# One-core perceiver layer: the passage from attention to the experts reordered, with seven tiles' routing tables made on GpSimd

## The reference

```python
p1 = jnp.cumsum(m1, axis=-2) - m1              # place among those that chose the same expert first
m1 = m1 * (p1 < C)
p2 = jnp.cumsum(m2, axis=-2) - m2 + m1_count   # second choices come behind the first ones
m2 = m2 * (p2 < C)
combine = c1 + c2                              # (token, expert, slot): the gate, 0 elsewhere
dispatch = (combine != 0)
expert_inputs = einsum('GSEC,GSM->EGCM', dispatch, x)
hidden = gelu(expert_inputs @ w0) * (expert_inputs @ w1)      # 1368 wide
out = einsum('EGCM,GSEC->GSM', hidden @ wo, combine)
```

## Time and profile before

| | |
|---|---|
| median of 3 runs (lowest, highest) | 552.87 us (552.48, 552.99) |
| the profiled execution | 554.64 us, span 552.5 us |
| granted TensorE clock, mean share | 0.944 |
| TensorE busy | 498.8 us, 90% of the span |
| VectorE, ScalarE, GpSimd busy | 400.5, 324.6, 254.5 us |

### The profile page before, as it was taken

The page is one execution under the profiler, slowest core; times in us unless marked ns, Lnnn a source line. Parts: engine busy times, 40 slices in busy tenths (PEclk is TensorE's granted clock), DMA queues, the critical chain, the costliest instruction groups (busy, mean ns, idle before and its releaser), DMA issues.

```text
span 552.5 us, 18285 instructions
## 1 busy us (share of the span) xinstructions
PE 498.8 (90%) x6637; PEld 457.4 (83%) x6637; DVE 400.5 (72%) x1003; ACT 324.6 (59%) x839; POOL 254.5 (46%) x349
## 2 busy tenths in 40 slices
PE   0888999999999999999966747999999999999996
PEld 0776888888888888888755536899999999999995
DVE  2444555666767766676777697599999999999963
ACT  1356777667757775775731216666666666666650
POOL 4134345344364344536310110566676666667650
PEclk9989999999999999999996655699999999999998
DMA  6623211201101110100017000344655656457202
GB/s 163 182 77 89 42 40 31 54 21 43 41 20 38 39 39 19 39 20 3 3 45 264 1 1 0 114 145 165 192 160 166 212 191 189 126 185 229 79 1 76
DMA packets 58125, 48.91 MB, mean 89 GB/s; under 512 B 20942, under 2 KB 49744, under 8 KB 58064
## 3 DMA queue, kind: packets, MB, share of 16 engines
q1 hardware_dynamic: 58064, 48.09, 30.3%
HBM read 46.86 MB, written 1.08 MB: 87 GB/s over the span
## 4 chain that ended last, share of the span: by engine, by line
PE 79%; ACT 5%; issue 5%; DVE 5%; DMA 3%; SPq 2%; ACTq 0%; DVEq 0%
PE bank L222 20%; PE bank L224 18%; PE bank L223 18%; PE bank L605 5%; PE bank L629 3%; PE bank L583 3%; PE bank L540 2%; ACT Pr L1058 2%; DMA w_raw<-in_L_xattn_Wk 2%; PE bank L760 2%; PE bank L988 2%; SPq L417 1%; ACT PTd L1151 1%; DMA last_prob<-Pr 1%; PE bank L722 1%
## 5 line engine op out<-in xcount | busy, mean ns | idle before, releaser
L222 PE MATMUL bank<-XT_lo,W_hi 128*128 128x256 f32 (+1 forms) x352 | 100.7, 286 | 1.3 <-ACT CT L1252 1.3
L223 PE MATMUL bank<-XT_hi,W_lo 128*128 128x256 f32 (+1 forms) x352 | 100.2, 285 | 0.0
L224 PE MATMUL bank<-XT_hi,W_hi 128*128 128x256 f32 (+1 forms) x352 | 100.0, 284 | 0.0
L2001 POOL TENSOR_TENSOR W_lo<-raw,W_hi 128x256 fp32r<-128x256 f32 (+1 forms) x88 | 87.8, 998 | 7.0
L1919 POOL TENSOR_TENSOR Pr<-Pr 128x1024 f32<-128x1024 f32 x31 | 58.8, 1897 | 48.8 <-DVE Pr L1401 48.0
L1058 ACT ACTIVATE Pr<-Sc,nmax 128x257 f32<-128x257 f32 x128 | 63.8, 502 | 23.1 <-DVE nmax L1392 20.1
L1392 DVE CUSTOM_DVE_ANT_0 Sc<-bank,mask_add 128x257 f32<-128x257 f32 x128 | 47.0, 423 | 40.3 <-PE bank L583 18.0
L1999 POOL CAST W_hi<-raw 128x256 fp32r<-128x256 f32 (+1 forms) x88 | 39.4, 447 | 75.0 <-PE bank L224 38.0
L1817 DVE TENSOR_TENSOR W_lo<-raw,W_hi 128x512 fp32r<-128x512 f32 (+1 forms) x88 | 69.6, 793 | 5.1 <-ACT W_hi L1225 1.4
L1847 DVE TENSOR_TENSOR hid_lo<-hid,hid_hi 128x256 fp32r<-128x256 f32 (+1 forms) x88 | 71.9, 818 | 1.5 <-ACT hid_hi L1301 1.5
L222 PEld LDWEIGHTS bank<-XT_lo,W_hi 128*128 128x128 f32 (+1 forms) x352 | 66.7, 190 | 1.6 <-issue 1.6
(11 more groups left out here) (238 smaller groups left out, 1331.3 us busy)
## 6 DMA issues: line engine op xcount, KB each, us to landing
raw<-in_L_ffn_w_kernel SPq DMA_DIRECT2D x32, 512.0 KB, 4.6
ctx_raw<-in_ctx SPq DMA_DIRECT2D x32, 256.0 KB, 2.8
raw<-in_L_ffn_wo_kernel SPq DMA_DIRECT2D x16, 512.0 KB, 5.7
raw<-in_L_ffn_w_kernel SPq DMA_DIRECT2D x16, 344.0 KB
last_prob<-Pr SPq DMA_DIRECT2D x128, 1.0 KB
raw<-in_L_ffn_wo_kernel SPq DMA_DIRECT2D x8, 256.0 KB
x_sb<-in_x SPq DMA_DIRECT2D x4, 256.0 KB, 6.4
VL_all<-vl_rows SPq DMA_DIRECT2D x8, 128.0 KB
```

The lines of the kernel that those rows point to most:

```text
L222: pe.matmul(dst, a_hi, b_lo, start=first, stop=False)
L223: pe.matmul(dst, a_lo, b_hi, start=False, stop=False)
L224: return pe.matmul(dst, a_hi, b_hi, start=False, stop=last)
L2001: po.tensor_tensor(W2_lo[0:w, m % RW, :], raw2[0:w, t, :], f(W2_hi[0:w, m % RW, :]), ALU.subtract)\
```

## The change

The calls of the stretch are put in another order on TensorE, VectorE, ScalarE and GpSimd, and several pieces of work change their engine or their bank. By parts:

- `normalise_last` goes into the last step of the loop, right behind `spread_probs` of tile 5; ScalarE multiplies two of the four groups and VectorE two. Before, VectorE multiplied all four after the loop.
- The values of tiles 6 and 7 are projected into a bank of their own (`self_values_at`), so that they need not wait for the rotation to have read queries and keys; `project_self(y_, True)` goes into the loop's last step.
- `spread_probs(y_)` is made by ScalarE alone, in four blocks; `scale_probs(y_)` goes from VectorE to GpSimd.
- Tiles 5 and 6 are chosen and placed together, in the form that tiles 0 to 4 had (`shift_group`, `share_group`, `choose_group`, `leave_first`, `place_group`); tile 7 keeps the single form.
- `add_weights(t)` on GpSimd takes the place of `weigh(t)` and `disperse(t)` for tiles 0 to 6. VectorE keeps both for tile 7. There are four `disp` buffers in the place of two.
- The turning of the weights of tiles 4 to 7 goes behind the first products of the feed-forward, and VectorE copies the low inputs of tile 7.

```diff
+        def add_weights(t):
+            po.wait_ge(sm["r_placed"], group_of(t) + 1)
+            if t >= 1:
+                po.wait_ge(sm["r_weighed"], t)
+            po.tensor_scalar(halves_[:, :], slot_no, slot_of[:, 1, one(t)], gate[:, 1, one(t)], ALU.is_equal, ALU.mult)
+            po.tensor_scalar(tile_of(C_all, t), slot_no, slot_of[:, 0, one(t)], gate[:, 0, one(t)], ALU.is_equal, ALU.mult)\
+              .then_inc(sm["r_halves"], 1)
+            po.wait_ge(sm["r_halves"], t + 1)
+            po.tensor_tensor(tile_of(C_all, t), tile_of(C_all, t), halves_[:, :], ALU.add).then_inc(sm["r_weighed"], 1)
+            po.wait_ge(sm["r_weighed"], t + 1)
+            if t >= 4:
+                po.wait_ge(sm["r_x_made"], t - 3)
+            po.tensor_scalar(disp_of(t), tile_of(C_all, t), 0.0, None, ALU.is_gt).then_inc(sm["r_disp"], 1)
...
         def normalise_last():
+            ve.wait_ge(sm["p_normed"], B - 1)
             ve.wait_ge(sm["p_inv"], B)
             r = (B - 1) % 2
-            ve.tensor_tensor(Pr[:, r, :, 0:2 * P], Pr[:, r, :, 0:2 * P], Pr[:, r, :, SC:SC + 1].broadcast_to([P, G, 2 * P]),
+            ve.tensor_tensor(Pr[:, r, 2:G, 0:2 * P], Pr[:, r, 2:G, 0:2 * P], Pr[:, r, 2:G, SC:SC + 1].broadcast_to([P, G - 2, 2 * P]),
                              ALU.mult).then_inc(sm["p_normed"], 1)
...
+        def normalise_last():
+            ac.wait_ge(sm["p_normed"], B - 1)
+            ac.wait_ge(sm["p_inv"], B)
+            r = (B - 1) % 2
+            for g in range(2):
+                last = ac.activation(Pr[:, r, g, 0:2 * P], Pr[:, r, g, 0:2 * P], ACT.Copy, scale=Pr[:, r, g, SC:SC + 1])
+            last.then_inc(sm["p_normed"], 1)
...
+                    if isinstance(j, int) and j == TT - 1:
+                        project_self(j - 1, True)
...
         turn_qk(z)
+        scores(z)
         self_outputs(y_)
-        scores(z)
...
+        def self_values_at(t):
+            return bk[5][:, D:2 * D] if isinstance(t, int) and t >= TT - 2 else bk[6][:, 0:D]
...
-            if t > 0:
-                ve.wait_ge(sm["r_weighed"], t)
             ve.tensor_scalar(second[:, :], slot_no, slot_of[:, 1, one(t)], gate[:, 1, one(t)], ALU.is_equal, ALU.mult)
...
-        for n in range(3):
-            split(0, n)
+        split(0, 0)
+        keep_low_inputs(z)
+        split(0, 1)
+        split(0, 2)
...
         up(*place(1))
+        turn_weights_of(2)
         for m in range(ALL):
             up(*place(m + 2))
             down(*place(m))
+            if m == 0:
+                turn_weights_of(3)
```

More of the change, by code:

```diff
@@ L685, in project_self @@
                 return
-            if of_values:
+            if of_values and isinstance(t, int) and t == TT - 2:
+                pe.wait_ge(sm["v_ready"], B)
+            elif of_values and isinstance(t, int) and t == TT - 1:
+                pe.wait_ge(sm["a_lT"], TT)
+            elif of_values:
                 pe.wait_ge(sm["b_cos"], t + 1)
@@ L701, in turn_qk @@
             pe.wait_ge(sm["b_rope"], t + 1)
[L702 removed]
+            if not isinstance(t, int) or t < TT - 2:
+                pe.wait_ge(sm["b_v"], t + 1)
             for i in range(4):
@@ L968, in down @@
                     pe.wait_ge(sm[by], max(EQ * half_ + q, 1))
+                if half_ == 0 and q == 1:
+                    pe.wait_ge(sm["ct_read"], 4)
             for h in range(SP_):
@@ L1149, in spread_probs @@
                 ac.wait_ge(sm["b_oT_made"], t)
-            for b in range(2):
+            for b in range(blocks):
                 last = ac.activation(PTd[b * S:(b + 1) * S, :, :, b, :],
@@ L1198, in step @@
                     keep_logits(j - 3)
+                if u == 3 and isinstance(j, int) and j == TT - 1:
+                    normalise_last()
                 keep_probs(b - 1, (u - 1) % 4)
@@ L1542, in spread_probs, with chain, follow @@
             last.then_inc(sm["b_pT_dve"], 1)
-        def chain(t, n, ins):
+        def chain(n, ins):
             ins.then_inc(sm["r_dve"], 1)
-            ve.wait_ge(sm["r_dve"], PICK * (t - EARLY) + n)
-        def follow(t, n, ins):
+            ve.wait_ge(sm["r_dve"], n)
+        def follow(n, ins):
             ins.then_inc(sm["r_slot"], 1)
-            ve.wait_ge(sm["r_slot"], PLACE * (t - EARLY) + n)
+            ve.wait_ge(sm["r_slot"], n)
         count = [0]
@@ L1605, in place_early @@
                                             op0=ALU.is_lt, op1=ALU.mult))
+            ve.sem_inc(sm["r_placed"], 1)
         def read_logits(t):
@@ L1614, in choose @@
         def choose(t):
-            ve.wait_ge(sm["r_neg"], t - EARLY + 1)
+            ve.wait_ge(sm["r_neg"], 1)
             first, last = lowest[:, 0, one(t)], lowest[:, 1, one(t)]
-            chain(t, 1, ve.scalar_tensor_tensor(out=tile_of(pick, t), in0=tile_of(lg, t), scalar=least[:, one(t)], in1=expert_no,
+            chain(1, ve.scalar_tensor_tensor(out=tile_of(pick, t), in0=tile_of(lg, t), scalar=least[:, one(t)], in1=expert_no,
                                                 op0=ALU.is_equal, op1=ALU.mult))
-            chain(t, 2, ve.tensor_reduce(first, tile_of(pick, t), X, ALU.min))
+            chain(2, ve.tensor_reduce(first, tile_of(pick, t), X, ALU.min))
@@ L1621, in choose @@
             ve.tensor_scalar(tile_of(chosen[:, 0], t), expert_no, first, None, ALU.is_equal)
-            ve.wait_ge(sm["r_exp"], t - EARLY + 1)
-            chain(t, 3, ve.scalar_tensor_tensor(out=tile_of(rest, t), in0=expert_no, scalar=first, in1=tile_of(exps_, t),
+            ve.wait_ge(sm["r_exp"], 1)
+            chain(3, ve.scalar_tensor_tensor(out=tile_of(rest, t), in0=expert_no, scalar=first, in1=tile_of(exps_, t),
                                                 op0=ALU.not_equal, op1=ALU.mult))
-            chain(t, 4, ve.tensor_reduce(gate[:, 1, one(t)], tile_of(rest, t), X, ALU.max))
@@ L1626, in choose @@
-            chain(t, 5, ve.scalar_tensor_tensor(out=tile_of(pick, t), in0=tile_of(rest, t), scalar=gate[:, 1, one(t)],
+            chain(4, ve.tensor_reduce(gate[:, 1, one(t)], tile_of(rest, t), X, ALU.max))
+            chain(5, ve.scalar_tensor_tensor(out=tile_of(pick, t), in0=tile_of(rest, t), scalar=gate[:, 1, one(t)],
                                                 in1=expert_no, op0=ALU.is_equal, op1=ALU.mult))
-            chain(t, 6, ve.tensor_reduce(last, tile_of(pick, t), X, ALU.min))
+            chain(6, ve.tensor_reduce(last, tile_of(pick, t), X, ALU.min))
@@ L1641, in slots_of @@
+            follow(2, ve.tensor_tensor(tile_of(pos2, t), at_[:, E:2 * E], tile_of(pos2, t), ALU.add))
             ve.sem_inc(sm["turns_ve"], 1)
@@ L1649, in slots_of @@
                                     op0=ALU.mult, op1=ALU.add)
[L1650 removed]
+            follow(4, ve.scalar_tensor_tensor(out=both(gate), in0=both(place_), scalar=float(CAP), in1=both(gate),
                                                  op0=ALU.is_lt, op1=ALU.mult))
         def weigh(t):
[L1655 to L1657 removed]
             ve.tensor_scalar(second[:, :], slot_no, slot_of[:, 1, one(t)], gate[:, 1, one(t)], ALU.is_equal, ALU.mult)
[L1659 removed]
+            follow(5, ve.tensor_scalar(tile_of(C_all, t), slot_no, slot_of[:, 0, one(t)], gate[:, 0, one(t)],
                                         ALU.is_equal, ALU.mult))
[L1661 removed]
+            ve.tensor_tensor(tile_of(C_all, t), tile_of(C_all, t), second[:, :], ALU.add).then_inc(sm["r_slot"], 1)
         statistics(0)
@@ L1705, in step @@
                     add_and_norm(j - 1, "b", 0)
+                ending = isinstance(j, int) and j == TT - 1
+                if ending and u == 3:
+                    invert_sums(B - 1, u)
+                    normalise_last()
+                    rotate(j - 1)
                 keep_probs(b - 1, (u - 1) % 4)
@@ L1709, in step @@
                 elif u == 3:
-                    rotate(j - 1)
+                    if not ending:
+                        rotate(j - 1)
                     split_self(j - 2)
```

274 lines of the change are left out of this document (140 added, 134 removed).

## The result

The change took 547.43 us (median of 16 runs) where the kernel before took 552.93 (16 runs): a ratio of 0.9909, 95% interval 0.9890 to 0.9929, or 5.0 us (3.9 to 6.1). The ratio is estimated from the runs in the chip's faster state and is not the quotient of the two medians, which is 0.9901. The forecast was 10.1 us. The sign is right and the time lies in the wide range of 537.0 to 549.5, but outside the forecast's own range of 539 to 546, and half of the gain is missing. The profiled execution took 548.07 us with a span of 546.3 (before 552.5).

A forecast was written before the change was run, and what follows sets the result against it. VectorE's queue was taken to bound the stretch before the feed-forward, with GpSimd idle beside it. First product 11.7 us earlier, less 1.6 given back, makes 10.1: 552.87 to 542.8 us; own range 539 to 546, wide range 537.0 to 549.5.

The forecast's parts named there:

- (a): Last block's probabilities at the loop's end: their turn on TensorE goes from 283.78 to about 280.8, 3.0 us earlier.
- (b): Cross projection of tile 7 on TensorE starts at 287.6 instead of 289.97, 2.4 us earlier.
- (c): Scores of tile 7 at 301.7 instead of 305.90, 4.2 us earlier; GpSimd's first weights start near 303.
- (d): Sum of tile 7 on VectorE at 315.0, 4.6 us earlier; its norm at 317.2, 6.6 us earlier.
- (e): Router's end on VectorE: places of tiles 5 and 6 at 326.8, with 2.0 us added for a busy GpSimd.
- (f): Weights and table on GpSimd: four steps of 0.72, 2.9 us a tile (1.9 to 3.9); last table at 332.6.
- (g): Last table to first feed-forward product: 3.4 us instead of 4.73, so the product at 336.0, 11.7 us earlier.
- (h): Turnings of tiles 4 to 7, now between the feed-forward's matrix products, give back 1.6 us.
- rival in which GpSimd becomes the bound: First product at 311 + 7w, w being GpSimd's us per tile; kernel slower from w = 5.0; chance 0.09.
- VectorE held up: Router's two-tensor VectorE steps lose 0.47 each beside GpSimd; (e) grows by 7.5 instead of 2.0; 548.3 us; chance 0.15.

## Why the forecast was half right

Each step of the forecast beside the row after; the last column adds the 1.1 us by which the loop ended earlier.

| step | forecast | measured | + 1.1 |
|---|---|---|---|
| (a) turn of the last probabilities | 280.8 | 279.36 | 280.5 |
| (b) cross projection of tile 7 | 287.6 | 286.29 | 287.4 |
| (c) scores of tile 7; first weights | 301.7; 303 | 300.99; 302.29 | 302.1; 303.4 |
| (d) sum of tile 7; its norm | 315.0; 317.2 | 314.77; 319.38 | 315.9; 320.5 |
| (e) places of tiles 5 and 6 | 326.8 | 327.95 | 329.1 |
| (f) a tile on GpSimd; last table | 2.9; 332.6 | 4.2; 337.59 | 338.7 |
| (g) from there to the first product | 3.4; 336.0 | 3.2; 340.80 | 341.9 |
| (h) turnings given back | 1.6 | 0.7 | |

(a) to (c) and the sum of tile 7 hold within 0.9 us: the order brings what it was to bring. That the stretch with all tables on VectorE is shorter by the same 11.7 us that the forecast had for the first product is a coincidence; the forecast's 11.7 has seven tables on GpSimd in it.

(f) is the step that failed, by the size of one term, the price of a tile on GpSimd. I had three rows and took the two-input step of the same size, 0.72; the two weight steps took 1.23 and 1.22 and the table step 0.86, each of them above it. The sum 1.23 + 1.22 + 0.73 + 0.86, with the gaps, is 4.2, beyond even the upper bound of 3.9. The Trainium skill (GPSIMD Engine Reference, 4.1 Engine selection) has one-input work at roughly line rate on GpSimd; these rows disagree: GpSimd took 1.23 for a step that VectorE wrote in 0.41. The nearest row was no neighbour in kind: a compare with a multiplication is not a cast, and no row of before had a scalar step at all.

The rest follows from the price. The late norm in (d) and the places in (e) come of it, since the power stood behind tile 2's weights; I had named this wait, for 3.9 us a tile. (e) itself was too long by 1.0: from the norm to the places it had 9.6 us and 8.6 were measured, with some 1.6 for the busy GpSimd where it had 2.0. With the power earlier the places were done at 325.98, on time. But that was not what the end waited for: at 2.9 a tile, the queue was to be free at 324, ahead of the places; at 4.2 it is free 0.9 behind them, and from there two tiles take 8.7 us instead of 5.8. GpSimd begins when the forecast said, at 302.29, and from there its queue has hardly a gap: the end is its sum. So with the 1.1 added the last table is 6.1 us late: 2.3 for the places, 0.9 for the queue behind them, 2.9 for the two tiles. The first product is 5.9 late, 11.7 becomes 5.8, and less the 0.7 of (h) that is 5.1, which agrees with the 5.0 measured.

The rival in which GpSimd becomes the bound was right in its mechanism and its formula: 311 + 7w gives 340.4 at w = 4.2, and 340.80 was measured. Its sign came by half: tile 7's power did wait in GpSimd's queue, but a scalar step took 1.23, not over 1.4, and the point from which the kernel is slower, w = 5.0, was not reached. It had been given a chance only on the side where it is slower; the price between 3.9 and 5.0, where the bound has moved and the kernel is still faster, had hardly any. VectorE held up: single steps of it are longer, as the 0.74 and 0.70 above where others of the kind take 0.17, but its line lost some 1.6 us in all, not 7.5, and the places came on time once the power did, so this rival fell. (h): the two turnings take 0.90 and 0.60, in part beside the products that follow, and the stage behind the first product is 0.7 longer; with 202.8 to 205.5 us for it in the experiments that is too small to judge.

## What to carry to other kernels

Before work moves to an idle engine, ask what one instruction of exactly that kind costs there; where no row of the trace shows it, an experiment of one instruction is worth more than three neighbouring rows. An idle engine at a third of the speed is worth only the work that it finishes before the others need it: seven tiles of eight were too many here. Three had the shortest stretch, but the times don't show that three are better than none. And a change of two parts should be forecast and run as two: here the rest of the change, its order above all, gave 11.7 us of one profiled stretch, and the move took 5 to 6 back.
